# Attention pass: SyncE fetches the 17 single rows of each share into a buffer of their own and hands the extra lanes' rows over in two parts

## The reference

```python
xl = (h @ Wl + bl).reshape(n, H, C)
xr = (h @ Wr + br).reshape(n, H, C)
e = jax.nn.leaky_relu(xl[dst] + xr[src], NEG_SLOPE)
logit = jnp.einsum('ehc,hc->eh', e, att)
m = jax.ops.segment_max(logit, dst, num_segments=n)
ex = jnp.exp(logit - m[dst])
den = jax.ops.segment_sum(ex, dst, num_segments=n)
alpha = ex / (den[dst] + 1e-16)
out = jax.ops.segment_sum(alpha[..., None] * xr[src], dst, num_segments=n)
```

## Time and profile before

| | us |
|---|---|
| median of 3 runs | 5737.38 (5736.91 to 5743.67) |
| the profiled execution's own time | 5733.8 |
| its span | 5731.7 |
| DVE busy in it | 4068.1 (71%) |
| PE busy / weight loads | 3638.7 (63%) / 3144.2 (55%) |
| POOL busy | 2966.9 (52%) |
| ACT busy | 1470.8 (26%) |

### The profile page before, as it was taken

The page is one execution under the profiler, slowest core; times in us unless marked ns, Lnnn a source line. Parts: engine busy times, 40 slices in busy tenths (PEclk is TensorE's granted clock), DMA queues, the critical chain, the costliest instruction groups (busy, mean ns, idle before and its releaser), DMA issues. The chain is left out here.

```text
span 5731.7 us, 121544 instructions
## 1 busy us (share of the span) xinstructions
PE 3638.7 (63%) x28023; PEld 3144.2 (55%) x28024; DVE 4068.1 (71%) x8991; ACT 1470.8 (26%) x3625; POOL 2966.9 (52%) x3112
## 2 busy tenths in 40 slices
PE   6887886455555553555565544555555555999985
PEld 5774443355545543545455534555555444999984
DVE  8998523677777777777777777777777657777754
ACT  4775200011111111111111110111111211555553
POOL 0000000566766753767766717767667204777773
PEclk9998997577777776677877766777777777999997
DMA  5883452244434432334444423444434222555552
GB/s 154 220 220 105 129 142 70 67 106 104 104 101 100 105 88 61 99 100 100 104 106 104 103 50 93 104 102 102 102 101 102 56 56 71 144 145 144 144 137 74
DMA packets 528864, 618.70 MB, mean 108 GB/s; under 512 B 123778, under 2 KB 465602, under 8 KB 528740
## 3 DMA queue, kind: packets, MB, share of 16 engines
q0 software_dynamic: 110400, 232.13, 17.7%
q10 hardware_dynamic: 254649, 235.22, 13.8%
q1 hardware_dynamic: 163691, 149.87, 10.0%
HBM read 521.60 MB, written 91.69 MB: 107 GB/s over the span
## 5 line engine op out<-in xcount | busy, mean ns | idle before, releaser
L615 POOL DMA_INDIRECT rows<-row_table,now x2340 | 2269.7, 970 | 1791.3 <-issue 1498.4
L903 PE MATMUL sums<-both,hot 125*125 125x137 f32 x5376 | 1018.9, 345 | 902.1 <-DVE acc L1003 718.6
L903 PEld LDWEIGHTS sums<-both,hot 125*125 125x125 f32 x5376 | 871.5, 235 | 985.3 <-DVE acc L1003 555.4
L600 POOL DMA_INDIRECT rows<-node_table,now x700 | 664.0, 949 | 507.6 <-issue 504.9
L893 PE MATMUL zp<-parts,hot_t 125*125 x8100 | 790.0, 263 | 206.4 <-DVE z L982 110.4
L893 PEld LDWEIGHTS zp<-parts,hot_t 125*125 125x125 bf16 x8100 | 756.0, 173 | 241.2 <-issue 239.6
L835 ACT CAST hot<-hot 125x500 f32<-125x500 bf16 x672 | 408.7, 608 | 1818.0 <-PE sums L903 1630.9
L982 DVE TENSOR_TENSOR z<-zp,rows 125x528 f32<-125x528 f32 x672 | 475.6, 708 | 489.6 <-issue 158.8
L995 DVE TENSOR_TENSOR both<-rows,turn 125x512 f32 (+1 forms) x672 | 457.2, 681 | 89.6 <-issue 46.3
L1278 PE MATMUL mixture<-row_parts,at 125*125 125x384 bf16 x2500 | 446.1, 330 | 45.2 <-DVE at L1335 45.2
L988 DVE TENSOR_REDUCE both<-z 125x16 f32<-125x512 f32 x672 | 457.3, 680 | 4.4
(11 more groups left out here) (467 smaller groups left out, 4588.8 us busy)
## 6 DMA issues: line engine op xcount, KB each, us to landing
hot_t<-hots_t ACTq DMA_DIRECT2D x902, 122.1 KB
hot<-hots ACTq DMA_DIRECT2D x896, 122.1 KB
counts<-pairs SPq DMA_DIRECT2D x55, 685.1 KB
rows<-row_table,now POOLq DMA_INDIRECT x2340
spread_slots<-slot_table POOLq DMA_DIRECT2D x56, 488.3 KB, 5.3
hots_t<-hot_t SPq DMA_DIRECT2D x112, 218.8 KB
hots<-hot_dst SPq DMA_DIRECT2D x112, 218.8 KB
pairs<-cells SPq DMA_DIRECT2D x25, 685.1 KB
```

What stands on the lines that cost most here:

```text
L600: pool.indirect_dma_start(rows[:, q, j, :], None, table, bass.IndirectOffsetOnAxis(ap=now[:, n, lane + j:lane + j + 1], axis=0)).then_inc( ...
L615: pool.indirect_dma_start(rows[0:lanes, q, j, :], None, table, bass.IndirectOffsetOnAxis(ap=now[0:lanes, n, lane + j:lane + j + 1], axis=0 ...
L903: ins = pe.matmul(sums[:, p, 0:ACCW], hot32[:, p, j * P:(j + 1) * P], values[:, p, j, :], start=j == 0, stop=j == HALF - 1)
```

## The change

All of it is in `pass_wide`, with one buffer and two semaphores more in `attention`. What POOL, DVE, PE and ACT are told to do stays the same.

- The 17 single rows are no longer written into the slot of turn 9 but into a buffer `alone`. SP loads their indices and issues their DMAs in turns 0 to 5: three in each of turns 0 to 4, two in turn 5.
- Each of the three hand-over DMAs is cut in two: in turn 7 the 28 rows of turns 0 to 6, in turn 8 the 8 rows of turns 7 and 8.
- In turn 8, after the second part, SP waits until the 17 rows have landed (`fetched`) and issues one DMA, SBUF to SBUF, from `alone` to the slot of turn 9. Turn 9 waits for seven DMAs on `given` in place of 20.

```diff
-    early = ALONE // 2 + 1
+    soon = GIVING - 2
+    each_turn = -(-ALONE // soon)
-    def hand_over(q):
+    def hand_over(q, lo, hi):
         for e in range(EXTRA):
-            sp.dma_start(rows[GIVERS * e:GIVERS * (e + 1), q, HALF - 1, :],
-                         rows[P + e:P + e + 1, q - GIVING:q, :, :]...).then_inc(given[q // SHARE], 16)
+            sp.dma_start(rows[GIVERS * e + HALF * lo:GIVERS * e + HALF * hi, q, HALF - 1, :],
+                         rows[P + e:P + e + 1, q - GIVING + lo:q - GIVING + hi, :, :]...).then_inc(given[q // SHARE], 16)
-    def fetch_alone(share, q, lo, hi):
+    def fetch_alone(share, parity, lo, hi):
             lane = EXTRA * GIVERS + lo + n
-            sp.dma_start(rows[lane:lane + 1, q, HALF - 1, :], table[bass.ds(v, 1), :]).then_inc(given[q // SHARE], 16)
+            sp.dma_start(alone[lane:lane + 1, :], table[bass.ds(v, 1), :]).then_inc(fetched[parity], 16)
@@ quads(i)
-                sp.wait_ge(given[share], landed(i, EXTRA + ALONE))
+                sp.wait_ge(given[share], landed(i, 2 * EXTRA + 1))
             sp.sem_inc(here, 1)
-            if turn == GIVING - 1:
-                hand_over(q + 1)
-                fetch_alone(RING // SHARE * i + share, q + 1, early, ALONE)
-            if turn == GIVING - 2:
-                fetch_alone(RING // SHARE * i + share, q + 2, 0, early)
+            if each_turn * turn < ALONE:
+                fetch_alone(RING // SHARE * i + share, share, each_turn * turn, min(each_turn * (turn + 1), ALONE))
+            if turn == soon:
+                hand_over(q + 2, 0, soon)
+            if turn == soon + 1:
+                hand_over(q + 1, soon, GIVING)
+                sp.wait_ge(fetched[share], landed(i, ALONE))
+                sp.dma_start(rows[EXTRA * GIVERS:P, q + 1, HALF - 1, :], alone[EXTRA * GIVERS:P, :]).then_inc(given[share], 16)
@@ attention
+        alone = sc.sb("alone", [P, ROW])
+        fetched = [sc.sem(f"fetched{n}") for n in range(RING // SHARE)]
```

More of the change, by code:

```diff
@@ L616, in gather_wide, with pass_wide @@
                                         bass.IndirectOffsetOnAxis(ap=now[0:lanes, n, lane + j:lane + j + 1], axis=0)).then_inc(rows_in[q], 16)
-def pass_wide(nc, sp, g, table, rows, now, lone, lone_in, staged, rows_in, given, here, kept, step_done, held_up):
-    early = ALONE // 2 + 1
-    assert HELD >= GIVING + SHARE - 1 and RING - HELD <= GIVING - 6
+def pass_wide(nc, sp, g, table, rows, now, lone, lone_in, alone, fetched, staged, rows_in, given, here, kept, step_done, held_up):
+    soon = GIVING - 2
+    each_turn = -(-ALONE // soon)
+    assert HELD >= GIVING + SHARE - 1 and RING - HELD <= SHARE - soon and each_turn * soon >= ALONE
     def stage(n, group):
@@ L630, in free @@
         sp.sem_inc(kept, 1)
-    def hand_over(q):
+    def hand_over(q, lo, hi):
         for e in range(EXTRA):
-            sp.dma_start(rows[GIVERS * e:GIVERS * (e + 1), q, HALF - 1, :],
-                         rows[P + e:P + e + 1, q - GIVING:q, :, :].rearrange("p a j f -> p (a j) f")).then_inc(given[q // SHARE], 16)
-    def fetch_alone(share, q, lo, hi):
+            sp.dma_start(rows[GIVERS * e + HALF * lo:GIVERS * e + HALF * hi, q, HALF - 1, :],
+                         rows[P + e:P + e + 1, q - GIVING + lo:q - GIVING + hi, :, :].rearrange("p a j f -> p (a j) f")).then_inc(given[q // SHARE], 16)
+    def fetch_alone(share, parity, lo, hi):
         _, at = nc.values_load_multi_w_load_instructions(lone[0:1, bass.ds(ALONE * share + lo, hi - lo)], engines=(sp.engine,), min_val=0, max_val=N - 1,
@@ L816, in _ @@
         def _(sp):
-            pass_wide(nc, sp, g, table, rows, now, lone, lone_in, staged, rows_in, given, here, kept, weighted, fetching)
+            pass_wide(nc, sp, g, table, rows, now, lone, lone_in, alone, fetched, staged, rows_in, given, here, kept, weighted, fetching)
         @block.scalar
```

## The result

The changed kernel takes 5686.65 us (median of 4 runs, 5684.51 to 5690.03) against 5737.15 us before (4 runs, 5733.05 to 5743.67). The ratio is 0.9911, 95% interval 0.9894 to 0.9929: 50.5 us faster. Predicted were 5689 us. The profiled execution has a span of 5682.4 us (5731.7 before), so it differs by 49.3 us, and all of it can be looked for in the trace.

A forecast was written before the change was run, and what follows sets the result against it. Late quads, caused by SP's issuing, were taken to cost the three passes 50.9 us (3140.6 - 3 x 1029.9). Leaving 3 aside gave -48 us, so 5737.4 - 48 = 5689 us, range 5682 to 5714.

The forecast's parts named there:

- Clean pass: One of the three passes, from first to last `z`, if no quad were late: 1029.9 us.
- the 3 us left aside: Part of the 50.9 us not counted as gain, for phases without enough reserve (block 1) and the later `given`.
- SP's two holds: SP's issuing delays `kept`, for which POOL waits (5.6 us a share), and `here` of turn 9, for which DVE waits.
- full and partial recovery: Late quads vanish (5689 us, chance 0.72), or turn 9 stays late and about half the loss remains (5712 us, 0.13).
- the slower cases: SP sets the pace (5990 us, chance 0.03), TensorE's clock falls (5763 us, 0.03), or another slowdown (0.02).
- the fetch turns: SP's turns 0 to 5, with index load, single-row DMAs and `free`: 3.6 us, 4.8 with the upper load, below 6.5.
- Theory A: Put to test in the follow-ups: POOL loses its reserve to the late `kept`; the prediction gave this most room.
- Theory B: Put to test in the follow-ups: `here` of turn 9 is late by itself, though its gathers have long landed.
- Under 60 us: Sign in the new profile: POOL's wait for `kept` (line 630), 292.8 us before, falls under 60 and stands behind a softmax.
- Turn 9 did not stay late: Rival: the hop through `alone` takes 2 to 3 us more, so turn 9 still trails DVE; 5712 us, chance 0.13.
- SP did not become the pace: Rival: fetch turns exceed the 5.3 us a quad has in DVE's mean, so every pass grows; 5990 us, chance 0.03.
- TensorE's clock did not fall: Rival: the clock drops to 1.2 GHz (0.5) throughout, PE's work outlasts each phase by 1.9 us; 5763 us, chance 0.03.

The follow-up runs named there:

- fetch_only: Changed kernel with the three 36-row hand-over DMAs left whole in turn 8, the single rows still fetched through `alone` in turns 0 to 5: 5686.17 us, ratio 0.9912.
- late_here: Changed kernel, but in turn 9 SP frees the next quad, then fetches six unused rows and waits for them before adding to `here`: 5736.01 us, ratio 0.9999.
- held_17: Kernel before with `HELD` 17 in place of 18, so each turn of SP allows POOL to begin quad q+3, not q+2: 5752.27 us, ratio 1.0023.
- kept_first: Kernel before, with SP freeing the next quad ahead of its hand-over and single-row issues in turns 7 and 8: 5790.11 us, ratio 1.0091.
- split_only: Kernel before with the hand-over cut in two (turns 7 and 8), the 17 rows still fetched straight into the slot: 5872.7 us, ratio 1.0231.
- pause_after_here: Changed kernel, but after `here` in turn 9 SP twice fetches seven unused rows, then waits for all 14: 5951.25 us, ratio 1.037.

## Why the prediction came out right, and where its reasoning didn't

**The bound and the sum.** Clean pass 1029.9 us, three passes 3140.6, so 50.9 us to be had: measured passes of 1029.4, 1031.1 and 1030.6 us, and 49.5 us gained. Of the 3 us left aside, 1.4 were needed. This step carried the number, and it holds whichever of SP's two holds cost the time. The chances don't quite add up: full and partial recovery are 0.85 together, where 0.86 is given for faster, and the slower cases are 0.08, where 0.07 is given.

**SP's turns.** Predicted 3.6 us for the fetch turns (measured medians 3.1 to 3.7), 3.8 for turn 7 (4.0), 2.7 to 3.8 for turn 8 (4.0: the copy took 0.63 us to issue, not 0.36, and the hand-overs of 8 rows 0.62 to 0.74 each, little less than 36 rows). The load of three indices was put at 0.83 us between 0.28 and 2.05 and took 0.84. The hop from `here` of turn 8 to that of turn 9 was put at 4.2 to 5.8 us and took 5.4 in the median. With the 1.0 us more that the prediction worked out from the Trainium skill's rule ("DMA: Bandwidth & Descriptors", section "Why a DMA increments its semaphore by 16 and not by 1": the number of engines has to divide the slowest dimension of both sides, so 17 partitions would go over one) it was 5.2 to 6.8. The median of 5.4 lies in both. But the single DMA packets in the trace bear the rule out: behind the copy's issue come 17 packets of 528 bytes one after the other, with one write to the semaphore for all of them, while each of the 24 packets of the hand-overs has its own. Where no other packets mix in (32 of the 60 shares) the 17 take 0.42 us from first to last, 25 ns each and not the 56 of the estimate, so that spreading them could have saved less than 0.42 us. Where turn 9 ends a phase (quads 99 and 199), its gathers end 8.3 us and its `here` comes 4.8 to 5.6 us ahead of its `z`.

**Which of SP's two holds cost the time.** The prediction named both: "POOL has no reserve left at the end of some phases", and SP withholds turn 9 though it has landed, and "SP's issuing is the cause of both". That SP's issues in turns 7 and 8 are the root is shown, as moving the single rows out of them brought the whole gain (fetch_only). How it divides is seen at single quads. Here are two of turn 9, each with the first `z` of its phase, its own last gather, and its own `z`, before the change and after it. Quad 169:

```profile
1913.69 0.71 DVE L982 TENSOR_TENSOR z<-zp,rows 125x528 f32<-125x528 f32 x1 [1.88 <-issue]
1955.81 1.19 POOL L615 DMA_INDIRECT rows<-row_table,now  x1 [0.30 <-SPq L630]
1967.79 0.71 DVE L982 TENSOR_TENSOR z<-zp,rows 125x528 f32<-125x528 f32 x1 [2.64 <-SPq L654]
```

```profile
1902.10 0.71 DVE L988 TENSOR_TENSOR z<-zp,rows 125x528 f32<-125x528 f32 x1 [1.88 <-issue]
1938.82 1.19 POOL L615 DMA_INDIRECT rows<-row_table,now  x1 [0.30 <-issue]
1953.77 0.71 DVE L988 TENSOR_TENSOR z<-zp,rows 125x528 f32<-125x528 f32 x1 [0.28 <-DVE both L997]
```

Quad 99:

```profile
1532.08 0.71 DVE L982 TENSOR_TENSOR z<-zp,rows 125x528 f32<-125x528 f32 x1 [1.88 <-issue]
1577.54 1.19 POOL L615 DMA_INDIRECT rows<-row_table,now  x1 [0.30 <-issue]
1589.50 0.71 DVE L982 TENSOR_TENSOR z<-zp,rows 125x528 f32<-125x528 f32 x1 [2.73 <-SPq L654]
```

```profile
1522.90 0.71 DVE L988 TENSOR_TENSOR z<-zp,rows 125x528 f32<-125x528 f32 x1 [1.88 <-issue]
1568.36 1.19 POOL L615 DMA_INDIRECT rows<-row_table,now  x1 [0.31 <-issue]
1577.87 0.71 DVE L988 TENSOR_TENSOR z<-zp,rows 125x528 f32<-125x528 f32 x1 [0.28 <-DVE both L997]
```

The gathers of quad 169 end 43.3 us into the phase before and 37.9 after, and its `z` stands at 54.1 and 51.7. In late_here and held_17 they end at 38.0 and 37.9, `here` comes 10.8 us behind them, as late as before (10.5), and `z` still stands at 51.7: where POOL is early, the late `here` costs nothing. That speaks for Theory A. The gathers of quad 99 end at 46.65 both times, and only `here` moved, from 10.5 us behind them to 3.3, which speaks for Theory B. Quads 28, 39, 69 and 199 of the first pass, late by 1.7 to 4.6 us before, are of the mixed kind: their gathers end 2.6 to 4.4 us earlier in the phase after the change.

An estimate of the division comes from putting both traces together. For each quad take the end of its gathers, counted from the first `z` of its phase, add the time from there to `here` and the 0.3 us in which a waiting `z` follows, and compare with the place of its `z` in a clean phase (quads whose `z` is the first of a phase are left out). The largest excess in each phase, summed over the three passes, is DVE's loss. From the trace before alone this gives 49.7 us, where the sums over single quads gave 49.5, and from that of late_here 47.7, where they gave 48.0.

| gathers end as in | `here` behind them as in | loss, us |
|---|---|---|
| before | before | 49.7 |
| after | before | 11.6 |
| before | after | 16.3 |
| after | after | 0 |
| late_here | late_here | 47.7 |
| after | late_here | 25.1 |

So by this estimate the late `here` alone would have cost 12 us and the held POOL alone 16, and freeing POOL alone, or making `here` prompt alone, would have given back some two thirds or more; the rest of the 50 us is there because both fall on the same quads, and a phase has only so much in hand. The estimate keeps each trace's times as they are, while in a real kernel POOL's times would shift with DVE's, and no run here has one hold without the other. late_here, held_17 and kept_first don't decide it: in each, the gathers of quad 99 end 4 us or more later in the phase than in the kernel before (50.6, 50.7 and 53.5 us), and its `here` stands as far behind them as before or further. How much one of the two alone would have given back stays open. What the prediction had too large is the size of POOL's gaps: it took 5.6 us a share from one share, 8.0 us a block, where the mean of the 60 shares is 4.0, or 5.7 us a block, just over the 5.1 to spare.

**POOL's wait.** "Under 60 us" contradicted the prediction's own sum: if POOL needs 70.8 us of each 75.9 it must stand 5.1 us in each of 42 blocks, 214 us, somewhere. It waits 236.0, now behind the ring: SP waits for DVE to use a quad up 464.3 us in all, where it was 238.6. The row of after:

```profile
SPq L631 <- DVE both L1001: 464.3, 110, 11.7
```

**The rivals.** Turn 9 did not stay late. SP did not become the pace; that more issuing or waiting in a single turn is dear is shown by split_only and pause_after_here, 136 and 265 us slower than the kernels that they were made from. TensorE's clock did not fall: three clean phases of after ran at 0.85, 0.83 and 0.75 granted (windows; PE, PEld, DVE, ACT, POOL), all 55 us, as the earlier trace rows had it for one at 0.75.

```profile
1295.10:1350.00 54.90, 33.91 (x288) 31.60 (x289) 43.29 (x88) 10.97 (x30) 40.01 (x41) 0.85 0.47 122
1370.90:1426.00 55.10, 35.55 (x290) 33.33 (x291) 43.38 (x89) 10.99 (x30) 40.05 (x42) 0.83 0.46 120
1522.90:1577.90 55.00, 38.02 (x285) 35.68 (x286) 43.37 (x89) 10.99 (x30) 39.98 (x42) 0.75 0.47 120
```

## What to carry to other kernels

When one queue both issues transfers and passes on "this is ready" and "this is free", follow single items through it: when the item was made, counted from the consumer's own clock (here the first step of a phase), and how long after that it was announced. Lateness is the sum of the two, so an experiment that restores only one of them may show the full loss or none of it, and an edit that is meant to touch one can move the other. Compare the same item in all traces before calling a cause isolated. A wait total on the producer (292.8 us here, 236.0 after, with the loss gone) says little.

Size such a gain from the consumer's clean stretches: that came within 2 us of the truth here without knowing how the two holds share it. A seemingly harmless move of issues onto the same queue can cost far more than it saves (split_only, 136 us), and a scheme that saves one gather in 40 should be weighed against none at all.

## What was unexpected of the hardware

An indirect gather with 125 lanes took 1.20 us on POOL and one with 128 lanes 0.94, in the same loop beside the same SP issues. With it, three of 39 gathers cost a share 0.75 us more, and the sharing saved 0.5 us of 50.0 in place of 1.25.

SP's load of registers went by 0.28 us for one value, 0.84 for three, and 0.92 to 2.21 for eight or nine. The short ones of the long loads come with every fourth share, where the first index stands at a multiple of four values. That the alignment is the cause is inferred from this pattern and wasn't tried.

A hand-over DMA of 8 rows took SP 0.62 to 0.74 us to issue, one of 36 rows 0.71 to 0.85, a single row 0.22: the number of rows mattered little.
